# Cross-attention with a gated FFN on one core: new banks in the opening, own orders for the first round, other places for a load, a cast and the last reciprocal roots

## The reference

```python
def _layernorm(x, eps=1e-5):                 # and a second one inside, with gamma and beta
    return (x - mean(x)) / sqrt(var(x) + eps)

def xattn(x, context, gamma, beta, w_q, w_kv, w_out, b_out, gate):
    xn = layernorm(x) * gamma + beta
    q = xn @ w_q
    k, v = split(context @ w_kv)
    attn = softmax(q * 64 ** -0.5 @ k.T)     # per head
    return (attn @ v @ w_out + b_out) * tanh(gate)

def ffn(x, w_gate, w_up, w_down):            # weights are integers / 127
    return (silu(x @ wg.T) * (x @ wu.T)) @ wd.T

x = x + xattn(_layernorm(x), ctx, ...)
x = x + ffn(_layernorm(x), ...)
```

## Time and profile before

| what | value |
|---|---|
| time, median of 3 runs | 296.05 us (295.01 to 296.74) |
| profiled execution: its own time | 297.51 us |
| profiled execution: span | 295.7 us |
| granted TensorE clock, mean | 0.994 |
| PE busy | 285.9 us (97%) |
| DVE / POOL / ACT busy | 231.1 / 172.1 / 158.8 us |

### The profile page before, as it was taken

One profiled execution on the slowest core, in us unless ns is written; L12 is line 12 of the kernel. 1 busy time (PEld: TensorE's weight loads), 2 busy tenths in 40 slices (PEclk: granted clock), 3 DMA queues, 4 the chain that ended last, 5 costly groups with the idle time before them and its releaser, 6 DMA issues.

```text
span 295.7 us, 6752 instructions
## 1 busy us (share of the span) xinstructions
PE 285.9 (97%) x2509; PEld 262.9 (89%) x2509; DVE 231.1 (78%) x609; ACT 158.8 (54%) x312; POOL 172.1 (58%) x198
## 2 busy tenths in 40 slices
PE   8999999979999999999999999999999999999895
PEld 7998978868988898989898989898999889988794
DVE  1598887777898789878987897788878878886853
ACT  4646875548268633853484358326842773354142
POOL 2653864358959681966396549635872778145033
PEclk9999999999999999999999999999999999999979
DMA  6995147332432113011201120112012101110001
GB/s 198 384 368 153 34 115 243 147 97 109 145 107 80 24 32 97 0 40 43 73 0 40 42 73 2 39 53 59 3 41 76 35 3 42 41 34 2 0 26 51
DMA packets 26668, 23.32 MB, mean 79 GB/s; under 512 B 12602, under 2 KB 24866, under 8 KB 26634
## 3 DMA queue, kind: packets, MB, share of 16 engines
q1 hardware_dynamic: 26634, 22.86, 24.9%
HBM read 15.87 MB, written 4.62 MB: 69 GB/s over the span
## 4 chain that ended last, share of the span: by engine, by line
PE 86%; DVE 6%; ACT 2%; issue 2%; SPq 1%; DMA 1%; POOL 1%; DVEq 0%
PE ps L904 13%; PE ps L849 10%; PE ps L808 6%; PE ps L816 5%; PE ps L812 5%; PE ps L973 5%; PE ps L977 5%; PE ps L974 5%; PE ps L738 5%; PE ps L831 4%; PE ps L957 3%; PE ps L960 3%; PE ps L925 2%; PE ps L771 1%; PE ps L746 1%
## 5 line engine op out<-in xcount | busy, mean ns | idle before, releaser
L1224 POOL TENSOR_TENSOR probs<-probs,total 128x512 f32<-128x512 f32 x32 | 33.6, 1049 | 59.6 <-DVE total L1363 59.5
L1250 POOL TENSOR_TENSOR h_lo<-hid,h_hi 128x256 fp32r<-128x256 f32 x42 | 30.9, 737 | 29.9 <-ACT h_hi L1137 29.5
L1239 POOL TENSOR_TENSOR t_lo<-t_all,t_hi 128x1232 fp32r<-128x1232 f32 x16 | 45.6, 2852 | 3.8 <-ACT t_hi L1095 3.8
L1067 ACT COPY pt<-ps 128x512 f32<-128x512 f32 x32 | 18.9, 591 | 40.8 <-PE ps L831 40.8
L973 PE MATMUL ps<-wo_hi,o_hi 128*128 128x256 f32 x128 | 36.3, 283 | 0.0
L974 PE MATMUL ps<-wo_lo,o_hi 128*128 128x256 f32 x128 | 36.1, 282 | 0.0
L977 PE MATMUL ps<-wo_hi,o_lo 128*128 128x256 f32 x128 | 36.0, 281 | 0.0
L1083 ACT CAST o_hi<-ps 128x512 fp32r<-128x512 f32 x32 | 17.2, 591 | 27.0 <-PE ps L849 27.0
L1346 DVE TENSOR_REDUCE top<-ps 128x4 f32<-128x308 f32 x64 | 28.7, 473 | 3.4 <-PE ps L816 3.1
L808 PE MATMUL ps<-t_hi,xn_hi 128*128 128x308 f32 x128 | 30.7, 321 | 0.0
L1371 DVE TENSOR_TENSOR o_lo<-ps,o_hi 128x512 fp32r<-128x512 f32 x32 | 20.6, 686 | 12.5 <-ACT o_hi L1083 12.2
(11 more groups left out here) (168 smaller groups left out, 838.2 us busy)
## 6 DMA issues: line engine op xcount, KB each, us to landing
x_ln<-in_x SPq DMA_DIRECT2D x8, 256.0 KB, 2.9
v_scratch<-v_out SPq DMA_DIRECT2D x4, 512.0 KB, 3.3
v_whole<-v_scratch SPq DMA_DIRECT2D x16, 128.0 KB
stream<-in_x SPq DMA_DIRECT2D x8, 256.0 KB, 2.9
x_rooms<-in_x SPq DMA_DIRECT2D x7, 256.0 KB, 7.7
out<-stream SPq DMA_DIRECT2D x7, 256.0 KB, 2.2
wk_raw<-in_L_xattn_w_kv SPq DMA_DIRECT2D x4, 256.0 KB, 5.2
wq_raw<-in_L_xattn_w_q SPq DMA_DIRECT2D x1, 1024.0 KB, 7.9
```

Source lines behind the costliest of these rows:

```text
L1224: nc.gpsimd.tensor_tensor(whole, whole, scale.to_broadcast([P, HR, HALVES, KEYS_WHOLE]), ALU.mult).then_inc(probs_done, 1)
L1239: nc.gpsimd.tensor_tensor(t_lo[:, :, cols], t_all[:, :, n, cols], t_hi[:, :, cols].bitcast(F32), ALU.subtract).then_inc(tlo_done, 1)
L1250: nc.gpsimd.tensor_tensor(h_lo[:, f, :], hid_of(b, f), h_hi[:, f, :].bitcast(F32), ALU.subtract).then_inc(hlo_done, 1)
```

## The change

1. T: jobs t0, t1, t2 take bank pairs 0, 2, 6, all later ones pairs 4, 2, 6, 0 by m mod 4; ACT copies 0 1 3 5 7 8 10 12 14 of 16 (before: 1 3 5 6 8 10 12 13 15).
2. v_rest of input 0: after value rows 1, 2, 3 are stored, 3, 3 and 2 of its 8 DMAs are issued (before 2, 0 and 6).
3. Round 0 has its own PE and DVE orders: T2 stands before G2, D0 before O0, H3 before M0, and Y0 moves from ACT to DVE, between M1 and R0.
4. ACT's stage X is split: the affine step stays `X`, the cast `xn_hi` becomes `XH`, and in rounds 1 to 6 the tanh `t0` stands between them.
5. End: tile 1's residual `R1` stands after na8 instead of after na11, and na9 to na11 alternate with nb0 to nb3; `la` moves from DVE to POOL; each tile has its own semaphore. PE does two plain 128x128 matmuls (`wu`, `keep_warm`) between xb and g0. The last down products are cut once more (`m0`, `m1`): four parts of tile 0, four of tile 1, then the fifth parts, then the sixth.

```diff
 PE_ORDER = "T0 S2 T1 X1T S3 V0 XT G0 G1 G2 T2 G3 S0 T3 G4 G5 V1 S1 O0 O1 D0 D1".split()
-ACT_ORDER = "Ta C0 C1 E2 X1 O0 X WO t0 t1 E3 t2 h0 C2 Tb t3 h1 C3 h2 t4 E0 h3 O1 h4 t5 h5 E1".split()
+ACT_ORDER = "Ta C0 C1 E2 X1 O0 X t0 XH WO t1 E3 t2 h0 C2 Tb t3 h1 C3 h2 t4 E0 h3 O1 h4 t5 h5 E1".split()
-ACT_FIRST = "Ta C0 C1 E2 O0 X E3 C2 WO C3 Tb E0 O1 E1 Y0 Y1".split()
+ACT_FIRST = "Ta C0 C1 E2 O0 X XH E3 C2 WO C3 Tb E0 O1 E1 Y1".split()
+PE_FIRST = "T0 S2 T1 X1T S3 V0 XT G0 G1 T2 G2 G3 S0 T3 G4 G5 V1 S1 D0 O0 O1 D1".split()
+DVE_FIRST = "M2 LN Z2 X1 M3 O0 H0 Z3 H1 H2 H3 M0 H4 O1 Z0 H5 M1 Y0 R0 Z1 R1 AG".split()
-PE_END = "O0.7 O1.7 G5.7 p0 p1 xa xb g0 q0 q1 g1 g2 g3 g4 g5 d0 d1 e0 e1".split()
+PE_END = "O0.7 O1.7 G5.7 p0 p1 xa xb wu g0 q0 q1 g1 g2 g3 g4 g5 d0 d1 m0 m1 e0 e1".split()
-DVE_END = ("... R0.7 na0 na1 na2 na3 na4 na5 na6 na7 na8 na9 na10 na11 R1.7 nb0 nb1 la nb2 nb3 "
+DVE_END = ("... R0.7 na0 na1 na2 na3 na4 na5 na6 na7 na8 R1.7 nb0 na9 nb1 na10 nb2 na11 nb3 "
...
-POOL_END = "P3.7 h0.7 h1.7 B.7 h2.7 h3.7 h4.7 h5.7 ..."
+POOL_END = "P3.7 h0.7 h1.7 B.7 h2.7 h3.7 h4.7 la h5.7 ..."
-ACT_TS = "1 3 5 6 8 10 12 13 15".split()
+ACT_TS = "0 1 3 5 7 8 10 12 14".split()
+T_BANKS_FIRST = (0, 2, 6)
+T_BANKS = (4, 2, 6, 0)
...
-                at = 2 * ((n - first_t) % 4)
+                m = n - first_t
+                at = T_BANKS_FIRST[m] if m < len(T_BANKS_FIRST) else T_BANKS[m % len(T_BANKS)]
...
                 if r == 1:
                     sp.wait_ge(s_vrow[0], 16)
                     load_v_whole(0)
-                    load_v_rest(0, 0, range(HR - 2))
+                    load_v_rest(0, 0, range(HR - 1))
+                if r == 2:
+                    load_v_rest(0, 0, range(HR - 1, HR))
+                    load_v_rest(0, 1, range(HR // 2))
                 if r == 3:
-                    load_v_rest(0, 0, range(HR - 2, HR))
-                    load_v_rest(0, 1)
+                    load_v_rest(0, 1, range(HR // 2, HR))
...
+            def keep_warm():
+                for _ in range(2):
+                    mm(ps[:, LAST_BANKS[0], 0:P], ident[:], ident[:], start=True, stop=True)
...
+            def split_x(n):
                 act.wait_ge(xn_done, DC * (n + 1))
                 if not (isinstance(n, int) and n == 0):
                     act.wait_ge(scores_done, 2 * NU * n)
                 nc.scalar.copy(xn_hi[:], xn[:]).then_inc(xnhi_done, 1)
...
+            def normalise_x1_first_tile():
+                pool.wait_ge(x2t_done, B - 1)
+                pool.wait_ge(ln_step, LN_STEPS * B)
+                nc.gpsimd.tensor_scalar(x1_hat[:, 0, :], residual_of(B, 1)[:, 0, :], mv[:, 0, 0:1], rstd[:, 0:1],
+                                        ALU.subtract, ALU.mult).then_inc(last_x1hat, 1)
```

More of the change, by code:

```diff
@@ L65 @@
            "t0.8 t1.8 h0.8 t2.8 h1.8 t3.8 h2.8 t4.8 h3.8 t5.8 h4.8 h5.8").split()
-DVE_END = ("Z3.7 H0.7 H1.7 H2.7 H3.7 H4.7 O1.7 R0.7 na0 na1 na2 na3 na4 na5 na6 na7 na8 na9 na10 na11 R1.7 nb0 nb1 la nb2 nb3 "
+DVE_END = ("Z3.7 H0.7 H1.7 H2.7 H3.7 H4.7 O1.7 R0.7 na0 na1 na2 na3 na4 na5 na6 na7 na8 R1.7 nb0 na9 nb1 na10 nb2 na11 nb3 "
            "nb4 nb5 nb6 nb7 nb8 nb9 nb10 nb11 lb xa H5.7 xb H0.8 Y0.7 H1.8 Y1.7 H2.8 H3.8 H4.8 H5.8 Y0.8 Y1.8").split()
-POOL_END = "P3.7 h0.7 h1.7 B.7 h2.7 h3.7 h4.7 h5.7 h0.8 h1.8 h2.8 h3.8 h4.8 h5.8".split()
+POOL_END = "P3.7 h0.7 h1.7 B.7 h2.7 h3.7 h4.7 la h5.7 h0.8 h1.8 h2.8 h3.8 h4.8 h5.8".split()
 PE_START = "v0 XT v1 v2 v3 S0 v4 FL S1 v5 v6 v7 v8 v9".split()
-ACT_START = "Ta X v0 v1 v2 v3 Tb v4 E0 v5 TG E1 v6 v7 v8 v9".split()
+ACT_START = "Ta X XH v0 v1 v2 v3 Tb v4 E0 v5 TG E1 v6 v7 v8 v9".split()
 DVE_START = "LN B0 B1 B2 BC M0 BR s4 M1 Z0 Z1 s5 s6 s7 BI".split()
 POOL_START = "XS F0 F1 F2 VZ Ta X Tb RZ P0 P1".split()
-ACT_TS = "1 3 5 6 8 10 12 13 15".split()
+ACT_TS = "0 1 3 5 7 8 10 12 14".split()
+T_BANKS_FIRST = (0, 2, 6)
+T_BANKS = (4, 2, 6, 0)
 STATS_AFTER = "k2 w0 w1 k3 k4 w2 t2 t3".split()
@@ L366, in xattn_ffn_kernel @@
         act_jobs += [copied_at[s] for s in ACT_FILLS]
-        dve_jobs += [copied_at[s] for s in DVE_ORDER if s in copied_at and s not in ACT_FILLS]
+        dve_jobs += [copied_at[s] for s in DVE_FIRST if s in copied_at]
         by_act = {n: i + 1 for i, n in enumerate(act_jobs)}
@@ L877, in transpose_x1_tile @@
             def transpose_x1_tile(t):
-                pe.wait_ge(x1hat_done, NT * (B - 1) + t + 1)
+                if t == 0:
+                    pe.wait_ge(last_x1hat, 1)
                 if t == 1:
+                    pe.wait_ge(x1hat_done, NT * (B - 1) + 1)
                     pe.wait_ge(x1_done, NT * B)
@@ L995, in stages_of @@
                     stages[f"q{t}"] = ("start", down_piece, B - 1, t, FC - 1, FC, general)
-                    stages[f"d{t}"] = ("start", down_piece, B, t, 0, FC - 1, general)
+                    stages[f"d{t}"] = ("start", down_piece, B, t, 0, FC - 2, general)
+                    stages[f"m{t}"] = ("start", down_piece, B, t, FC - 2, FC - 1, general)
                     stages[f"e{t}"] = ("start", down_piece, B, t, FC - 1, FC, general)
@@ L1000, in stages_of @@
                 stages["FL"] = ("start", transpose_largest)
+                stages["wu"] = ("start", keep_warm)
                 return stages
@@ L1137, in split_h @@
                 nc.scalar.copy(h_hi[:, f, :], hid_of(b, f)).then_inc(hhi_done, 1)
-            stages = {"X1": ("ffn", split_x2), "X": ("next", affine_x),
+            stages = {"X1": ("ffn", split_x2), "X": ("next", affine_x), "XH": ("next", split_x),
                       "Ta": ("next", split_t, 0), "Tb": ("next", split_t, 1)}
@@ L1265, in _ @@
                 stages[f"h{f}"] = ("ffn", split_h, f)
+            stages["la"] = ("start", normalise_x1_first_tile)
             stages["XS"], stages["XS2"] = ("start", x_scales, 0, FIRST_X), ("first", x_scales, FIRST_X, B)
@@ L1465, in scale_step_tile @@
                 col = slice(t, t + 1)
-                done = LN_STEPS * (B - 1 + t)
+                counted, done = (ln_step, LN_STEPS * (B - 1)) if t == 0 else (last_ln_step, 0)
                 if i == 0:
@@ L1472, in scale_step_tile, with normalise_last_tile @@
                     dve.wait_ge(aggr_done, NT * (B - 1) + t + 1)
-                    nc.vector.tensor_scalar(var_eps[:, col], mv[:, col, 1], EPS, None, ALU.add).then_inc(ln_step, 1)
+                    nc.vector.tensor_scalar(var_eps[:, col], mv[:, col, 1], EPS, None, ALU.add).then_inc(counted, 1)
                     return
-                dve.wait_ge(ln_step, done + i - 1)
+                dve.wait_ge(counted, done + i - 1)
                 if i == 2:
                     nc.vector.tensor_scalar(rstd[:, col].bitcast(I32), var_eps[:, col].bitcast(I32), -0.5, RSQRT_SEED,
-                                            ALU.mult, ALU.add).then_inc(ln_step, 1)
+                                            ALU.mult, ALU.add).then_inc(counted, 1)
                 elif i % 3 == 0:
-                    nc.vector.tensor_tensor(tmp[:, col], rstd[:, col], rstd[:, col], ALU.mult).then_inc(ln_step, 1)
+                    nc.vector.tensor_tensor(tmp[:, col], rstd[:, col], rstd[:, col], ALU.mult).then_inc(counted, 1)
                 elif i % 3 == 1:
                     nc.vector.scalar_tensor_tensor(tmp[:, col], tmp[:, col], -0.5, var_eps[:, col], ALU.mult,
-                                                   ALU.mult).then_inc(ln_step, 1)
+                                                   ALU.mult).then_inc(counted, 1)
                 else:
                     nc.vector.scalar_tensor_tensor(rstd[:, col], tmp[:, col], 1.5, rstd[:, col], ALU.add,
[L1486 to L1490, removed]
+                                                   ALU.mult).then_inc(counted, 1)
+            def normalise_last_tile():
+                dve.wait_ge(last_ln_step, LN_STEPS)
+                nc.vector.tensor_scalar(x1_hat[:, 1, :], residual_of(B, 1)[:, 1, :], mv[:, 1, 0:1], rstd[:, 1:2],
                                         ALU.subtract, ALU.mult).then_inc(x1hat_done, 1)
@@ L1514, in _ @@
                     stages[f"n{name}{i}"] = ("start", scale_step_tile, t, i)
+            stages["lb"] = ("start", normalise_last_tile)
             for b in range(FIRST_X, B):
```

11 lines of the change are left out of this document (6 added, 5 removed).

## The result

| | kernel before | changed kernel |
|---|---|---|
| time, median of 20 executions each | 296.15 us (295.01 to 298.08) | 294.71 us (294.50 to 295.67) |
| ratio, 95% interval | | 0.995 (0.9935 to 0.9965) |
| profiled execution: own time | 297.51 us | 294.75 us |
| profiled execution: span | 295.7 us | 292.9 us |
| granted TensorE clock, mean of that execution | 0.994 | 1.000 |

The kernel became 1.44 us faster. The forecast was 3.4 us, to 292.6. The direction and the range (290.5 to 295.3) were right, the size was not. The two profiled executions lie 2.76 us apart, nearly twice what the medians do. That difference between the two comparisons turned out to be the centre of this case.

A forecast was written before the change was run, and what follows sets the result against it. PE was taken as busy throughout the rounds, so gains lay in its waits. Terms -1.1 - 0.9 + 2.3 - 1.3 - 0.2 - 0.6 - 1.6 = -3.4 us, from 296.05 to 292.6 us; range 290.5 to 295.3.

The forecast's parts named there:

- against the median, 296.05 - 3.4: Final step: the summed -3.4 us, read from the profiled execution, subtracted from the median to give 292.6 us.
- the end of that fall: End, from 281.29 to g5's end: the clock's fall to 0.50 taken as gone, -1.6 us (bounds 0 and -1.6).
- v_rest: Round 0: loads issued sooner on SP remove V0's 0.88 us wait, -0.9 us (bounds 0 and -0.9).
- the smaller pieces: Last down products: PE does tile 1's eight matmuls while waiting for the fifth part's h_lo, -0.6 us.
- the rival in which one fall stays: One clock fall remains, at the end or after D0's wait: 292.6 + 1.7 = 294.3 us; chance 0.30.
- T's banks: T: third job's gap shrinks by 0.7 and v0's wait for DVE's copy by 0.4, -1.1 us.
- D0 before O0: Round 0: PE waits 1.8 us for bank 7's copy, plus 0.45 for transposes moved ahead, +2.3 us.
- t0 before the cast: Rounds 1 to 6: H0 ends about 0.6 us earlier, G3's wait for bank 3 goes, -1.3 us.
- The rival that T3's wait takes the gain: t0's gain goes to the next release, T3 waiting for POOL's probabilities: 293.9 us; chance 0.09.
- Roots and g0: End: xb's wait shrinks from 0.82 to 0.3; x2_lo of tile 1 then bounds g0, -0.2 us.
- A fall of its own after D0's wait: Round 0 projections: D0's 1.8 us wait can bring a clock fall, +1.7 us; taken as 0.

The follow-up runs named there:

- the first two series: Unchanged kernel before, timed beside the first four and the next four follow-ups, each on another chip: medians 296.33 us (29 executions) and 296.49 us (35).
- The tenth experiment: Changed kernel with only DVE's copy in H5's place moved from behind Z0 to ahead of O1, D0 still ahead of O0: 293.09 us, ratio 0.9894.
- the eleventh experiment: Changed kernel with D0 behind both projections, Y0 back on ACT, and the last tile's store issued from ACT's queue instead of SP's: 292.64 us, ratio 0.9883.
- series 3: Unchanged kernel before, timed beside the last four follow-ups on a third chip: median 296.13 us over 11 executions.
- the seventh experiment: Kernel before with only the v_rest loads of input 0 spread between the value rows' stores: 295.98 us, ratio 0.9982.

## Why the forecast came out half wrong

**The step that failed: "against the median, 296.05 - 3.4".** The sum was made from one execution that had the clock fall, own time 297.51, and 1.6 of the 3.4 us were the end of that fall. They were then subtracted in full from a median that had no fall in it. The warning stood in the table: the profiled execution was 1.46 us above the median and outside the range of the runs shown, its mean clock was 0.994, and the fall was priced at nearly the same amount. Subtracted from 297.51 the sum gives 294.1, against 294.75 measured. The price itself was a little high: PE's some 50 matmuls at 0.118 us make 5.9, but the held executions take some 6.1 for the same stretch, so a fall costs 1.4 to 1.5 and not 1.6, and 1.34 are in the table of moments. In the medians of all executions the fall was worth 0.4 and 0.5 us in the first two series (median of all less held), since 27 of 75 executions had it. Beside the changed kernel no clock of the kernel before is on record; with the held median of the other series it comes to 0.2 (296.15 - 295.97), an estimate. So this term alone is too large by more than 1.1 us, over half of the miss of 2.1.

Two more terms were too large in the time, v_rest by 0.5 and the smaller pieces by 0.6. That the measured 294.71 fell within the range, and near the 294.3 of the rival in which one fall stays, is luck in part: that end of the range was there for a fall after D0's wait or at the end, and neither came.

The rest, term by term (timeline; then time, held against held):

- **T's banks, -1.1:** -1.08 in the timeline, -1.18 alone. Right, with both of its parts: `v0` came 1.30 earlier, `XT` 1.14.
- **v_rest, -0.9:** -0.96 in the timeline, -0.4 alone. The mechanism was right. The size was that of one execution's landing time; the same loads in the same places made V0 wait between 0 and 0.88 us.
- **D0 before O0, +2.3 (1.8 and 0.45):** 1.69 of wait, 2.29 in all in the timeline, 1.86 and 2.35 by the two comparisons of times. The tenth experiment parts the two: the copy moved forward takes the wait away and leaves 0.47. DVE's order, not PE's, set the wait.
- **t0 before the cast, -1.3:** -1.51 in the timeline, -2.1 alone. The rival that T3's wait takes the gain is out: rounds of 28.28 in the changed kernel and with the edit alone.
- **Roots and g0, -0.2:** -0.28, though the wait before xb shrank to 0.51 and not to the 0.3 forecast. `la` took 1.24 us on POOL, and PE did not wait for it.
- **Smaller pieces, -0.6:** -0.46 up to the last matmul, nothing in the time: -0.23, -0.02 and +0.26 us in three comparisons (with against without). The stretch from the last matmul to the end took 3.80, 3.96, 4.0, 4.23, 4.14, 4.13 and 4.15 us in the profiles with the pieces, and 3.26, 3.28, 3.29, 3.4, 3.82, 3.73 and 3.66 without, 0.57 more in the mean. In the thirteen profiles in which SP issues both last stores, this stretch is always the time of their issue (0.95 to 1.89 us) plus 2.28 to 2.36 us. The issue took 1.47 to 1.89 us with the pieces and 0.95 to 1.50 without, so it tends to be longer with them but isn't theirs alone. Yet the eleventh experiment made both issues short and the stretch stayed. Why the end moves less than the last matmul stays open.
- **A fall of its own after D0's wait (part of the rival at 0.30):** it didn't come, the clock stood at 1.000 after 1.69 us without a matmul. The other part, that the fall at the end stays in spite of `wu` and the shorter waits, didn't come in the changed kernel either. `wu` alone gave no fall in 12 executions (12 of 29 had it in the kernel before, beside it), the shorter waits without `wu` none in 11. With both, 2 of 61 executions of seven kernels still had it, so it is rare and not gone (24 of the 61 ran beside series 3, in which the kernel before had it only once).

Set against the held median, with the measured values in place of the forecast's, the single edits give -1.18 (T) - 0.4 (v_rest) - 1.5 (rounds) - 0.3 (roots and g0) + 0 (pieces) + 1.9 to 2.35 (D0) = -1.0 to -1.5, and -1.26 was measured. For t0 this takes the timeline's 1.5; with the 2.1 that the edit gave alone, the sum is -1.6 to -2.1 and 0.4 to 0.8 us too large, so the single edits add up to the whole only to within that much. Why a kernel whose order is fixed has the fall in some executions and not in others stays open: the waits before g0 were the same.

## What to carry to other kernels

A sum read from one profile belongs to that execution. Before it is subtracted from a median, each term has to be asked whether the median execution has it; an own time above the range of the runs, with a clock under 1, says that it likely hasn't. When a stage is moved ahead, look for who holds its bank and where that reader stands in the other engine's order: here DVE's copy in its old place cost 1.7 us of PE's time, and one moved word in DVE's order gave 1.6 of the measured time back. And a large change should be costed so that its losing part can be dropped: five parts of six gained or were neutral, one lost, and without that one the gain is more than twice as large.

## What the runs showed of the hardware

- The clock fall is not a property of the kernel alone: 27 of 75 executions of the same program had it, 12 of 29 and 14 of 35 on two chips and 1 of 11 on a third, at 1.2 to 1.5 us each in the first two series. With the old waits before g0 and without `wu` five kernels had it in 43 of 123 executions. Two plain 128x128 matmuls between transposes and products, or waits shorter by a few tenths, made it rare: none in 12 and in 11 executions, and 2 of 61 with both.
- In the two profiled executions that had the fall, the clock stood at 0.50 from about 281.7 to 285.1 us (the kernel before, g0 at 280.74) and from about 281.1 to 284.5 (the seventh experiment, g0 at 279.47), by stretches of 0.5 us. Three others with the same busy time of PE ahead of g0, to 0.02 us, kept 1.00.
- One wait of 1.69 us in the middle of dense work left the clock at 1.00, while 1.28 us of idle time in 7.74 us, with no wait above 0.82, went ahead of the fall at the end of the kernel before. By the Trainium skill (TensorE: Matmul & The Clock Gate, Why this matters for your kernels) short gaps between bursts should keep the clock; the D0 wait agrees with it, the end of the kernel before differs, in some executions.
- Eight small loads from device memory in fixed places were the last thing ready by 0 to 0.88 us, and the issue of two equal stores at the end took from 0.95 to 1.89 us on SP. The time from the last matmul to the end of the span varied from 3.26 to 4.23 us.
